# A two-branch graph convolution on one Trainium2 core: finer first splits, GpSimd's adds behind the split, features in pairs

## The reference

```python
d = (sum(adj, axis=1) + 1e-09) ** -0.5
H_f = relu((d[:, None] * adj * d[None, :] @ x) @ W_f + b_f)
H_s = relu((d[:, None] * adj * d[None, :] @ spatial_x) @ W_s + b_s)
attn = sigmoid(concat(H_f, H_s) @ W_att + b_att)
out = layernorm(x + attn * H_f + (1 - attn) * H_s)
```

## Time and profile before

| what | value |
|---|---|
| median of three runs | 394.38 us |
| profiled execution | 394.35 us |
| span of its instructions | 392.6 us |
| TensorE busy | 376.2 us, 96% |
| VectorE busy | 303.9 us, 77% |
| ScalarE busy | 283.8 us, 72% |
| GpSimd busy | 161.8 us, 41% |
| block adds on GpSimd (line 840) | 40 in 69.2 us, 1730 ns each |
| splits on VectorE (line 494) | 86 in 159.5 us |
| splits on ScalarE (line 690) | 86 in 125.8 us |

### The profile page before, as it was taken

How to read it: one execution, slowest core, us unless ns; L and a number is a source line. 1 busy time by engine, 2 the same in 40 slices (tenths; PEclk the granted TensorE clock), 3 DMA queues, 4 the chain that set the end, 5 groups by cost and what they waited for, 6 DMA issues and landing times. The chain is left out here.

```text
span 392.6 us, 5474 instructions
## 1 busy us (share of the span) xinstructions
PE 376.2 (96%) x1778; PEld 314.7 (80%) x1778; DVE 303.9 (77%) x434; ACT 283.8 (72%) x364; POOL 161.8 (41%) x199
## 2 busy tenths in 40 slices
PE   7779999999999999999999999999999999999990
PEld 7668778778888888888888888888788888888990
DVE  2889996979668875959589593929977887888896
ACT  3777788788878887887868887878633566668464
POOL 2343601770067603782259200010000427787764
PEclk9999999999999999999999999999999999999996
DMA  7999999999999999999999999999575434354001
GB/s 276 424 416 423 419 419 424 418 422 419 422 417 422 425 417 423 417 422 422 419 422 419 414 416 421 417 416 390 222 276 191 192 124 187 126 194 122 28 28 54
DMA packets 24508, 130.77 MB, mean 333 GB/s; under 512 B 2848, under 2 KB 7840, under 8 KB 10400
## 3 DMA queue, kind: packets, MB, share of 16 engines
q1 hardware_dynamic: 24480, 130.43, 82.6%
HBM read 128.32 MB, written 2.10 MB: 332 GB/s over the span
## 5 line engine op out<-in xcount | busy, mean ns | idle before, releaser
L398 PE MATMUL sums<-Ah,Yh 128*128 128x512 f32 (+1 forms) x528 | 203.7, 386 | 5.4 <-DVE Yl L503 5.0
L400 PE MATMUL sums<-Al,Yh 128*128 128x512 f32 (+1 forms) x528 | 202.1, 383 | 0.0
L399 PE MATMUL sums<-Ah,Yl 128*128 128x512 f32 (+1 forms) x528 | 202.1, 383 | 0.0
L494 DVE TENSOR_TENSOR Al<-raw,Ah 128x2048 fp32r<-128x2048 f32 (+2 forms) x86 | 159.5, 1861 | 32.2 <-ACT Ah L690 32.2
L690 ACT ACTIVATE Ah<-raw 128x2048 fp32r<-128x2048 f32 (+2 forms) x86 | 125.8, 1475 | 50.4 <-DMA raw<-in_At 31.5
L398 PEld LDWEIGHTS sums<-Ah,Yh 128*128 128x128 f32 x528 | 99.2, 188 | 27.3 <-DVE Yl L503 6.6
L400 PEld LDWEIGHTS sums<-Al,Yh 128*128 128x128 f32 x528 | 99.2, 188 | 19.6
L399 PEld LDWEIGHTS sums<-Ah,Yl 128*128 128x128 f32 x528 | 99.3, 188 | 19.0
L700 ACT ACTIVATE nat<-nat 128x2048 f32<-128x2048 f32 (+1 forms) x54 | 100.1, 1854 | 19.8 <-DMA nat<-in_adj 19.1
L514 DVE TENSOR_TENSOR acc<-sums,acc 128x512 f32<-128x512 f32 (+1 forms) x122 | 78.3, 675 | 36.6 <-PE sums L400 36.6
L840 POOL TENSOR_TENSOR S<-S,raw 128x512 f32<-128x512 f32 x40 | 69.2, 1730 | 27.5 <-DMA raw<-in_At 24.3
(11 more groups left out here) (51 smaller groups left out, 135.7 us busy)
## 6 DMA issues: line engine op xcount, KB each, us to landing
raw<-in_At SPq DMA_DIRECT2D x63, 1024.0 KB, 9.0
nat<-in_adj SPq DMA_DIRECT2D x47, 1024.0 KB, 11.6
nat<-in_adj SPq DMA_DIRECT2D x8, 768.0 KB, 9.4
xs<-in_xs SPq DMA_DIRECT2D x7, 512.0 KB, 10.4
out<-xs SPq DMA_DIRECT2D x32, 64.0 KB, 1.6
nat<-in_adj SPq DMA_DIRECT2D x2, 512.0 KB, 6.9
raw<-in_At SPq DMA_DIRECT2D x2, 512.0 KB, 8.3
xs<-in_xs SPq DMA_DIRECT2D x2, 128.0 KB, 7.0
```

The source lines that it names most:

```text
L398: pe.matmul(to, Yh[:, t % YRING, hs], high, start=first, stop=False)
L399: pe.matmul(to, Yl[:, t % YRING, hs], high, start=False, stop=False)
L400: mm = pe.matmul(to, Yh[:, t % YRING, hs], low, start=False, stop=last)
L494: dve.tensor_tensor(Al[:, k % SPLITS, a * IB:b * IB], raw[:, k % RAWS, a * IB:b * IB], Ah[:, k % SPLITS, a * IB:b * IB], ALU.subtract).the ...
```

## The change

Items 1 to 19 are split in pieces of one, one and two blocks. The features of a tile still stand behind the first piece, which now is block 0 alone; the evictions that stood behind the first piece now stand behind the second. GpSimd's adds of item k wait until all four blocks of item k have been split. The features of tile 0 are loaded behind the first rows, and those of tiles 4 to 11 in pairs directly ahead of the item at which the pair's first tile falls due (tiles 4 and 5 at item 8, 6 and 7 at 11, 8 and 9 at 15, 10 and 11 at 19), in place of two loads of four tiles behind items 6 and 11.

```diff
-HALVED = 20
+STEPWISE = 20
...
-    X_AFTER = {y_position(m * GT) - (2 if m == 1 else 4): m for m in range(1, G)}
+    X_EARLY = [(0, 1), (1, 2), (2, 4), (4, 6), (6, 8), (8, 10), (10, 12)]
+    X_BEFORE = {y_position(a): i for i, (a, b) in enumerate(X_EARLY) if i >= 1}
+    X_AFTER = {y_position(m * GT) - 4: m for m in range(3, G)}
...
-            return [(0, 2), (2, GT)] if k < HALVED else [(0, GT)]
+            return [(0, 1), (1, 2), (2, GT)] if k < STEPWISE else [(0, GT)]
...
-            sp.dma_start(xs[:, 0:1, :], xs_v[0, :, 0:1, :]).then_inc(x_early[0], 16)
+            def load_x_early(i):
+                a, b = X_EARLY[i]
+                c = a % GT
+                sp.dma_start(xs[:, a:b, :], xs_v[a // GT, :, c:c + b - a, :]).then_inc(x_early[i], 16)
+
             for k in range(K):
                 for n in parts[k]:
                     load_part(n)
-                if k == 2:
-                    sp.dma_start(xs[:, 1:2, :], xs_v[0, :, 1:2, :]).then_inc(x_early[1], 16)
-                if k == 4:
-                    sp.dma_start(xs[:, 2:GT, :], xs_v[0, :, 2:GT, :]).then_inc(xs_sem[0], 16)
+                if k == 0:
+                    load_x_early(0)
+                if k in X_BEFORE:
+                    load_x_early(X_BEFORE[k])
                 load_item(k)
...
                         for r in y_at[k]:
                             y_low(r)
-                        if k < HALVED:
-                            evacuate_new(ending[:3])
+                    elif a == 1:
+                        evacuate_new(ending[:3])
...
             def sum_block(k, j):
                 g = runs[items[k][j][0]][0] - BY_COLUMN[0]
                 n = blocks_summed(k - 1) + summed_blocks(k).index(j)
                 raw_here(pool, k)
+                pool.wait_ge(low_ok, GT * (k + 1))
                 if n >= 1:
                     pool.wait_ge(block_sum_ok, n)
```

More of the change, by code:

```diff
@@ L165, in build @@
         y_at[y_position(r)].append(r)
-    X_AFTER = {y_position(m * GT) - (2 if m == 1 else 4): m for m in range(1, G)}
-    assert len(X_AFTER) == G - 1
+    X_EARLY = [(0, 1), (1, 2), (2, 4), (4, 6), (6, 8), (8, 10), (10, 12)]
+    X_BEFORE = {y_position(a): i for i, (a, b) in enumerate(X_EARLY) if i >= 1}
+    X_AFTER = {y_position(m * GT) - 4: m for m in range(3, G)}
+    assert len(X_BEFORE) == len(X_EARLY) - 1 and len(X_AFTER) == G - 3
     H_F, H_S, H_ALL = slice(0, H), slice(H, H2), slice(0, H2)
@@ L248, in build @@
         nat_in = [sem(f"nat_in{i}") for i in range(NATS)]
-        x_early = [sem("x_first"), sem("x_second")]
-        xs_sem = [sem(f"xs_in{i}") for i in range(G)]
+        x_early = [sem(f"x_early{a}") for a, b in X_EARLY]
+        xs_sem = {m: sem(f"xs_in{m}") for m in range(3, G)}
         const_in = sem("const_in")
@@ L615, in _ @@
                 ending = [e for e in evac_order if end_item[e] == k - 1]
-                if k < HALVED:
+                if k < STEPWISE:
                     evacuate_new(ending[:2])
@@ L625, in _ @@
                     if a == 0:
-                        if k >= HALVED and len(ending) == GT:
+                        if k >= STEPWISE and len(ending) == GT:
                             evacuate_new(ending[:2])
@@ L631, in _ @@
                             y_low(r)
-                        if k < HALVED:
-                            evacuate_new(ending[:3])
-                if k < HALVED or k in (FINAL - 1, FINAL):
+                    elif a == 1:
+                        evacuate_new(ending[:3])
+                if k < STEPWISE or k in (FINAL - 1, FINAL):
                     evacuate_new(ending)
@@ L710, in y_high @@
                 act.wait_ge(D_ok, r + 1)
-                if r < 2:
-                    act.wait_ge(x_early[r], 16)
+                if r < X_EARLY[-1][1]:
+                    act.wait_ge(next(x_early[i] for i, (a, b) in enumerate(X_EARLY) if r < b), 16)
                 else:
```

## The result

The changed kernel takes 410.25 us (median of five runs, 409.83 to 410.78) against 394.52, a ratio of 1.040 with a 95% interval of 1.0385 to 1.0416. It is 15.7 us slower; 5.1 had been forecast. The profiled execution took 410.6 us with a span of 408.8.

What follows compares the result with a forecast made beforehand. The prediction took TensorE to bound the kernel, so only its waits move the end. Its lag terms, from -0.3 at the start, summed to +5.1: 394.35 + 5.1 = 399.4 us, range 397.6 to 401.2.

Steps and rivals of the forecast that it cites:

- Start: Before the first item: tile 0's features loaded behind the first rows let row sums start earlier, -0.3 us.
- Tile 1: At item 2: TensorE gets the low half of tile 1's features earlier, 25.1 against 26.30 us, -1.2.
- Item 6: Tile 3's features: late adds and degree give back 0.7 us, leaving TensorE 0.5 ahead of before.
- Item 11: Tile 6's late features stand ahead of block 1: TensorE waits 1.9 us, lag +1.4 at item 12.
- Item 13 at no further price: Tile 7 repeats item 11: the old wait of 0.28 us stays and the lag stays +1.4.
- Items 19 and 20: Tile 10's late features cost 1.5 us inside item 19; ScalarE's list then delays item 20's split, 1.7 more.
- Item 21: Tile 11: the same chain after item 20's adds costs 0 to 1 us, taken as 0.5.
- After item 21: Whole splits and tiles used an item later: 0 us, at most 1; items 5.44 us apart from item 22.
- Raw slots: Loads waiting for later adds cost 0 us, at most 2, since the DMA queue holds work enough.
- One price at each place: Rival: ScalarE makes up its lateness before items 20 and 21; 397.2 us, chance 0.22.
- Loads starve: Rival: later raw slots empty the DMA queue in the saturated stretch; 402.5 us, chance 0.12.
- The freed VectorE wins: Rival: adds leave splits alone, degrees come in time and TensorE's waits go; 390.8 us, chance 0.07.

Runs made afterwards that it cites:

- e10: The changed kernel with 14 more warm-up matmuls ahead of the first item: 410.23 us.
- e2: The kernel before with only the wait on GpSimd's adds added: 410.65 us, ratio 1.041.
- e13: The changed kernel with four raw slots for three and the features of tiles 16 and 20 made one item later: 406.1 us.
- e14: The changed kernel with four raw slots, and from item 20 on degrees ahead of the adds of the item before: 403.01 us.
- e3: The changed kernel, wait kept, with GpSimd making an item's degrees ahead of the adds of the item before: 399.66 us.
- e6: The changed kernel with a fourth raw slot alone, 9 rows for 12 in the last stage's buffer: 409.5 us.
- e8: The kernel before with the features' loads alone changed: 394.29 us, ratio 0.9985 to 1.0003.
- e4: The kernel before with the splits in one, one and two alone: 394.03 us, ratio 0.9982 to 1.0001.
- e5: The changed kernel, wait kept, with degrees ahead of the adds of the item before and a fourth raw slot: 394.33 us.
- e12: The changed kernel without the added wait, with degrees ahead of the adds and four raw slots: 397.52 us.
- e1: The changed kernel without the added wait on GpSimd's adds: 393.80 us, ratio 0.9987.
- e7: The changed kernel without the added wait and with 14 more warm-up matmuls: 395.13 us.

## Why the prediction was wrong

The direction and the mechanism were right: the tile's degree behind adds that wait for the split. The size was a third of the measured one. The step that failed is the sum's treatment of lateness that is handed on: the prediction worked out ScalarE's list after a late D once, at item 20, and took it as nothing everywhere else. Of the 11.5 us between the measured lag of 16.6 and the forecast 5.1, 8.2 lie there: 1.7 behind item 12, 1.4 at item 21, 5.1 after it. Another 2.9 were there by item 2, most of it from the first item, where the clock fell.

- *Start, -0.3 forecast.* The changed kernel began 0.37 late and ran most of its first item at a granted clock of 0.50: a lag of 2.94 at item 1. The row sums did come earlier (D at 10.69 for 11.28), but with them the warm-up ended earlier, and TensorE stood idle for 2.98 us before item 0 and not 2.03. This term was not seen at all. At the end it is worth little: e10 took it away and the median did not move, and of the changed kernel's own runs the one with the highest mean granted clock (0.996, against 0.986 in the profiled one) took 409.83 us for 410.6.
- *Tile 1, -1.2 forecast.* Measured +1.65. The step from item 1 to item 2 gave back 1.29. Most of the miss is the clock, since the evictions of item 0 stand ahead of the split of item 1, and that ahead of the adds: e10, at full clock, starts item 2 at -0.42. Of the 0.8 that are left, 0.5 is the split of item 1, which ended at 20.56 there and not near 20.1.
- *Item 6, +0.7 forecast.* Measured from item 2 on: +0.83. Right in size; 0.60 of it is the longer stop before item 6.
- *Item 11, +1.9 forecast.* Measured 1.82 at item 12, with a stop of 1.52 inside the item. Right in size, but the reason given, that only one block is ready ahead of the late features, is not what costs: e2, with two blocks ready, loses 2.42 in the same step and 3.46 from item 19 to item 20. A second block that is ready moves the stop and does not shorten the chain.
- *Item 13 at no further price.* Measured +0.89, and +0.86 more at items 14 and 15. The same list of ScalarE's that I priced at item 20 ran here too: blocks and row sums behind tile 6's late half, so that the split of item 12 ended at 88.39 and the adds and tile 7's D behind it.
- *Items 19 and 20, 1.5 + 1.7 forecast.* Measured 3.54, with stops of 1.53 and 1.56. Right within 0.4.
- *Item 21, 0.5 forecast, 0 to 1.* Measured 1.76, and 1.89 by item 22: outside the bounds. The chain of items 18 to 20 comes round once more with ScalarE already late.
- *After item 21, "I take 0, at most 1".* Measured 5.1. This is the largest miss. The reason given, that the tile is used an item later, was true and beside the point: ScalarE waits for D in its own order, 4.61 us at tile 16, and the next item's whole split comes behind that. e13 shows it for two tiles, e14 for the stretch (nothing lost after item 22). The sign "from item 22 on items are 5.44 apart" thus failed, with stops before items 29, 31 and 39; the others came, later than forecast by the lag (tile 10's D at 127.72 for 123).
- *Raw slots, 0.* In e3 they are worth 5.3 us. In the changed kernel they are hidden behind the longer chain (e6 against the changed kernel: 0.75), so the term was right in the sum and wrong as a statement about the slots: the earlier trace rows showed waits that did no harm, not how much more would.
- *Features in pairs, 0; finer splits, 0.* e8 and e4: within 0.4 us. Right.
- *Rivals.* "One price at each place" failed the wrong way: from item 19 to item 21 ScalarE did not make up its lateness, as the stops before items 20 and 21 show (1.56 and 1.47). "Loads starve" was real, but only where the order is mended. "It cancels" is refuted by the time. "The freed VectorE wins" is refuted for the change as it stands: VectorE's work got shorter, and the degrees came late. The Trainium skill's rule ("SBUF — State Buffer", section "Who interferes with whom") fits the groups above, 1218 ns for 1306 and 528 for 698, and e5 against e12, 394.33 for 397.52, fits it too, without showing that the port is the cause.

The added pieces of the measured lag at item 48: 2.94 by item 1, -0.46 to item 6, 1.88 to item 12, 1.74 to item 16, 5.43 to item 22, 5.08 after: 16.6. The span is 16.2 longer; the last stage gets 0.4 back.

## What to carry to other kernels

When a wait is added to an engine that works in order, write down what stands behind the waiting instruction, and then behind that on the next engine, until the chain comes back to the engine that bounds: here GpSimd, ScalarE, VectorE, TensorE and, through the evictions, GpSimd again. Lateness that is worked out at one place has to be asked for at every place where the pattern returns, and an operand that is needed later does not help if the wait for it blocks work that is needed sooner. If an order can't keep up, put the short work that others wait for ahead of the long work that nobody does, and check that the buffers the long work holds are enough.

## What the hardware showed that was not expected

TensorE's granted clock in the first item fell to 0.50, the lower of its two levels, in the changed kernel, after an idle time of 2.98 us; in e1 it fell after 2.86 us and in e7, before item 2, after 3.12. It stayed at 1.00 after 2.03 us before the first item of the kernel before, and after 2.00 in e4. The length of the idle time alone does not tell it: in e2 it fell after 2.15 us, in e8 it stayed after 2.21. The same window in the middle of the first item, of the changed kernel, the kernel before, e2 and e8: six matmuls in 2 us at a granted clock of 0.50, ten at 1.00.

```profile
14.00:16.00 2.00, 2.00 (x6) 1.58 (x5) 1.41 (x4) 1.21 (x3) 0.00 (x0) 0.50 1.02 430
14.00:16.00 2.00, 2.00 (x10) 1.65 (x10) 2.00 (x4) 1.52 (x2) 1.39 (x2) 1.00 0.98 414
14.00:16.00 2.00, 2.00 (x6) 1.51 (x6) 1.58 (x3) 1.51 (x2) 0.00 (x0) 0.50 1.00 426
14.00:16.00 2.00, 2.00 (x10) 1.67 (x9) 2.00 (x5) 1.13 (x2) 1.15 (x1) 1.00 1.04 438
```
